# One transpose group and one activation change places in the last stage's instruction order

## The chip, the cores and the metric

The kernel runs on one core of one Trainium2 chip. The metric is the device time of one execution in microseconds (us), measured on the chip. Inside the core, TensorE (PE), VectorE (DVE), ScalarE (ACT), GpSimd (POOL) and SyncE (SP) each run their own list of instructions in the order in which it was written, and they meet only at semaphores.

## The reference

The input x has 16 batches of 256 rows with 256 columns. It passes four residual parts: a decayed running sum gated by x, a feed-forward layer whose operands are quantised to fp4, attention with 16 heads, and a second feed-forward layer whose operands are quantised to block floating point (blocks of 32 share an exponent, 3 mantissa bits). Only the last one matters here:

```python
def block_quant(v, m_bits, bk):              # blocks of bk along the last axis
    amax = max(abs(vb), axis=-1)             # vb: v cut into blocks
    scale = exp2(floor(log2(amax)) - m_bits)
    return round(vb / scale) * scale
h = block_quant(layernorm(x)) @ block_quant(w_fc).T + b_fc       # 256 -> 1024
h = gelu(h)
x = x + tanh(g) * (block_quant(h) @ block_quant(w_proj).T + b_proj)   # 1024 -> 256
```

## The kernel before, in words

All data of the 16 batches stays on the chip between the stages. There are three stages, one after the other: the running sum with the fp4 layer, the attention, and the last feed-forward layer. Each stage is written once per engine as a body for one batch; `over_batches` runs it for batches 0 to 15, the middle ones in a loop of two batches per turn. In the last stage batches 2 to 9 are in that loop. A body works on several batches at once, since it is a software pipeline: `b` is the batch whose hidden values are quantised in this body, `fwd` is b+2, `prv` is b-1.

The way of one batch through the last stage is this. VectorE takes the statistics of its rows (`ff_input_stats`), GpSimd the power, ScalarE normalises (`ff_norm`), VectorE finds block maxima (`ff_input_magic`), GpSimd adds the rounding constant (`ff_input_up`), VectorE subtracts it (`ff_input_codes`). TensorE transposes these codes (`ff_turn_input`, L696), ScalarE copies them out (`ff_input_out`, L999). TensorE multiplies them in four pieces of 512 columns (`ff_fc(b, 0)` to `ff_fc(b, 3)`, L709 and L711), and ScalarE applies gelu to each piece (`ff_gelu(b, u)`, L1005, into `f_h`). VectorE takes the block maxima of all four pieces at once and makes the constants (`ff_hidden_magic`, L1607 to L1614); its wait is for all four gelus: `dve.wait_ge(f_a_gelu, b.count(4, 4))`. GpSimd adds the constants (`ff_hidden_up`, L1214), VectorE subtracts them in two halves (`ff_hidden_codes`, L1623, two instructions). TensorE transposes each half (`ff_turn_hidden(b, 0)` and `(b, 1)`, L724), ScalarE copies each out (`ff_hidden_out`, L1011), TensorE multiplies by the second weights (`ff_proj`, L733 and L736), and VectorE adds the residual (`ff_add_ffn`, L1630).

The transposed input of batch b+3 shares a PSUM bank with the first half of the hidden transposes of batch b. Therefore `ff_turn_input(b+3)` waits until `ff_hidden_out(b, 0)` has copied that half out.

The order of VectorE in the body of b, which the change does not touch, is: the residual of b-2, a small shift for b+5, `ff_hidden_magic(b+1)`, the statistics of b+6, `ff_input_codes(b+3)`, the two halves of `ff_hidden_codes(b)`, `ff_input_magic(b+4)`. So the maxima that follow the gelus of body b (which are those of batch b+2) are the third item of VectorE's body b+1. GpSimd's order is `ff_input_up(b+3)`, `ff_hidden_up(b)`, the power for b+6. SP stores one finished batch per body. GpSimd's `ff_hidden_up(b)` writes a single buffer and so waits for the codes of b-1; `ff_gelu(b+2, 0)` waits for `ff_hidden_up(b)`, since `f_h` has two buffers.

Of the kernel before, what the change touches and what calls it, by code (L numbers as in the profile page):

```python
# [146 lines left out]
def build_main(nc, load, loaded, out_v, g_xattn, g_ffn, w_gate_up, w_down, w_fc, b_fc, w_proj, b_proj, ident, decay,  # L147
# [3 lines left out]
    with ExitStack() as keep:  # L151
# [274 lines left out]
        def _(pe):  # L426
# [260 lines left out]
            def ff_turn_input(b):  # L687
                pe.wait_ge(f_v_code, b.count(1, 1))
                if b.shifted(-1):
                    pe.wait_ge(f_a_x, b.shifted(-1).count(1, 1))  # L690
                if b.shifted(-3):
                    pe.wait_ge(f_a_h, b.shifted(-3).count(C, 1))
                bank = f_ps_x.bitcast(BF16)
                for kc in range(KD):
                    for c in range(C):
                        ins = nc.tensor.transpose(bank[:, (kc * C + c) * P:(kc * C + c + 1) * P],  # L696
                                                  f_xcode[:, b.par, c, kc * P:(kc + 1) * P], idb[:, :])
                ins.then_inc(f_t_x, 1)

            def ff_fc(b, u):  # L700
                c, half = u // 2, u % 2
                cols = slice(half * 512, (half + 1) * 512)
                if u == 0:
                    pe.wait_ge(f_a_x, b.count(1, 1))
                if b.shifted(-1):
                    pe.wait_ge(f_a_gelu, b.shifted(-1).count(4, u + 1))
                elif u >= 2:
                    pe.wait_ge(a_exp, SU * B)
                nc.tensor.matmul(f_ps_fc[u // 2][:, u % 2, :], ones3[:, :], bias3[:, cols], start=True, stop=False)  # L709
                for kc in range(KD):  # L710
                    ins = nc.tensor.matmul(f_ps_fc[u // 2][:, u % 2, :], f_xt[:, b.par, kc, c, :], w_fc_t[:, kc, cols],  # L711
                                           start=False, stop=kc == KD - 1)
                ins.then_inc(f_t_fc, 1)

            def ff_turn_hidden(b, c):
                pe.wait_ge(f_v_hcode, b.count(C, c + 1))
                if c == 0 and b.shifted(2):
                    pe.wait_ge(f_a_x, b.shifted(2).count(1, 1))
                if c == 1 and not b.shifted(-1):
                    pe.wait_ge(a_v_out, len(V_OUT) * B)  # L720
                if b.shifted(-1):
                    pe.wait_ge(f_a_h, b.shifted(-1).count(C, c + 1))
                for k in range(KH1):
                    ins = nc.tensor.transpose(f_ps_h[c][:, :].bitcast(BF16)[:, k * P:(k + 1) * P],  # L724
                                              f_hcode[:, b.par, c, k * P:(k + 1) * P], idb[:, :])
                ins.then_inc(f_t_h, 1)

            def ff_proj(b, c):
                if c == 0 and b.shifted(-1):
                    pe.wait_ge(f_v_y, b.shifted(-1).count(1, 1))  # L730
                if c == 0 and not b.shifted(-1):
                    pe.wait_ge(a_v_out, len(V_OUT) * B)
                nc.tensor.matmul(f_ps_o[:, c, :], ones3[:, :], bias3[:, I1:I1 + D], start=True, stop=False)  # L733
                pe.wait_ge(f_a_h, b.count(C, c + 1))
                for k in range(KH1):
                    ins = nc.tensor.matmul(f_ps_o[:, c, :], f_ht[:, b.par, c, k, :], w_proj_t[:, k, :],  # L736
                                           start=False, stop=k == KH1 - 1)
                ins.then_inc(f_t_o, 1)

            def ff_body(b):  # L740
                prv, fwd = b.shifted(-1), b.shifted(2)
                if fwd:
                    ff_fc(fwd, 0)
                    ff_fc(fwd, 1)
                if prv:
                    ff_proj(prv, 0)
                if fwd:
                    ff_fc(fwd, 2)
                if prv:
                    ff_proj(prv, 1)  # L750
                if fwd:
                    ff_fc(fwd, 3)
                ff_turn_hidden(b, 0)
                if b.shifted(3):
                    ff_turn_input(b.shifted(3))
                ff_turn_hidden(b, 1)
# [36 lines left out]
            for u in range(4):  # L793
                ff_fc(lead[1], u)
            ff_turn_input(lead[2])
            over_batches(pe, ff_body, FFN_AHEAD, FFN_BEHIND)
            ff_proj(last, 0)
            ff_proj(last, 1)

        @block.scalar  # L800
        def _(act):
# [185 lines left out]
            def ff_norm(b):  # L987
                act.wait_ge(f_v_shift, b.count(1, 1))
                if b.shifted(-2):
                    act.wait_ge(f_g_up, b.shifted(-2).count(1, 1))  # L990
                for c in range(C):
                    nc.scalar.activation(f_xn[:, b.par, c * D:(c + 1) * D], tiles(xres, b)[:, c, :], ACT.Identity,
                                         bias=f_shift[:, b.par, c:c + 1], scale=f_rstd[:, b.par, c:c + 1]).then_inc(f_a_norm, 1)

            def ff_input_out(b):
                act.wait_ge(f_t_x, b.count(1, 1))
                if b.shifted(-2):
                    act.wait_ge(f_t_fc, b.shifted(-2).count(4, 4))
                nc.scalar.copy(f_xt[:, b.par].rearrange("p a c t -> p (a c t)"), f_ps_x.bitcast(BF16)).then_inc(f_a_x, 1)  # L999

            def ff_gelu(b, u):
                act.wait_ge(f_t_fc, b.count(4, u + 1))
                if u == 0 and b.shifted(-2):
                    act.wait_ge(f_g_hup, b.shifted(-2).count(1, 1))
                nc.scalar.activation(f_h[:, b.par, u * 512:(u + 1) * 512], f_ps_fc[u // 2][:, u % 2, :], ACT.Gelu).then_inc(f_a_gelu, 1)  # L1005

            def ff_hidden_out(b, c):
                act.wait_ge(f_t_h, b.count(C, c + 1))
                if b.shifted(-2):
                    act.wait_ge(f_t_o, b.shifted(-2).count(C, c + 1))  # L1010
                nc.scalar.copy(f_ht[:, b.par, c].rearrange("p k t -> p (k t)"), f_ps_h[c][:, :].bitcast(BF16)).then_inc(f_a_h, 1)  # L1011

            def ff_body(b):
                fwd = b.shifted(2)
                if fwd:
                    ff_gelu(fwd, 0)
                    ff_gelu(fwd, 1)
                if b.shifted(5):
                    ff_norm(b.shifted(5))
                if fwd:  # L1020
                    ff_gelu(fwd, 2)
                    ff_gelu(fwd, 3)
                ff_hidden_out(b, 0)
                if b.shifted(3):
                    ff_input_out(b.shifted(3))
                ff_hidden_out(b, 1)

            act.dma_start(idf[:, :], ident).then_inc(const_loaded, 16)
# [41 lines left out]
            ff_input_out(lead[2])  # L1070
            ff_norm(lead[4])
            over_batches(act, ff_body, FFN_AHEAD, FFN_BEHIND)

        @block.gpsimd
# [695 lines left out]
```

## Time and profile before

| | |
|---|---|
| median of 3 runs | 823.79 us (823.54 to 824.48) |
| profiled execution, its own time | 823.79 us |
| span of its trace | 821.7 us |
| mean granted TensorE clock | 0.937 |
| busy: PE / DVE / ACT / POOL | 704.8 / 691.7 / 486.3 / 431.6 us |
| last stage | about 669 us to the end of the span |

The span runs from the first instruction to the last; the profiled execution's own time is 2.1 us longer. Busy time is an average over three stages with different limits, so the last stage has to be read by itself.

### The profile page before, as it was taken

To read this page: it belongs to the slowest core of one execution; us is meant where nothing else is said; L and a number is where in the kernel's file an instruction comes from. 1 tells how busy PE (TensorE), PEld (TensorE's weight loads), DVE (VectorE), ACT (ScalarE), POOL (GpSimd) and SP (SyncE) were. 2 spreads that over 40 slices of the span, in tenths; PEclk is the share of its full clock that TensorE was granted. 3 is DMA by queue.
4 is the path that set the end of the run, shared out by engine and by line. 5 is a ranking of instruction groups with operands and counts; after the bars stand their busy time and mean duration, and the time that the engine had idled before them with its cause. 6 is when DMAs were issued, how large, how long until landed. Compare 5 with 4: busy or idle time off the path is not lost.

```text
span 821.7 us, 16554 instructions
## 1 busy us (share of the span) xinstructions
PE 704.8 (86%) x5075; PEld 517.6 (63%) x5090; DVE 691.7 (84%) x1230; ACT 486.3 (59%) x955; POOL 431.6 (53%) x331
## 2 busy tenths in 40 slices
PE   2365999999999998689999999999999876787785
PEld 1254888888888886566666666666666433455454
DVE  6856888888888878878999999998998649999995
ACT  3343455454555442428878887788878684656653
POOL 3623656646566555745444455555443516666553
PEclk9776999999999999889999999999999796989898
DMA  8710000000000000001000000000001000100011
GB/s 275 231 46 0 1 1 1 0 0 0 0 0 1 1 0 2 1 13 41 2 3 2 1 1 1 1 2 1 1 1 53 2 1 0 37 28 26 27 39 52
DMA packets 17719, 18.35 MB, mean 22 GB/s; under 512 B 1670, under 2 KB 16912, under 8 KB 17680
## 3 DMA queue, kind: packets, MB, share of 16 engines
q1 hardware_dynamic: 17084, 17.66, 6.6%
q8 instruction: 21, 0.34, 0.2%
q10 hardware_dynamic: 596, 0.20, 0.1%
q14 instruction: 18, 0.15, 0.1%
HBM read 13.39 MB, written 4.19 MB: 21 GB/s over the span
## 4 chain that ended last, share of the span: by engine, by line
PE 57%; DVE 20%; issue 9%; ACT 5%; POOL 3%; DMA 3%; DVEq 1%; SPq 1%; POOLq 0%; ACTq 0%
PE ps_o L540 9%; PE a_ps_pv L635 7%; PE a_ps_t L579 7%; PE a_ps_s L620 6%; PE a_ps_m L599 5%; DVE f_ps_small L1607 4%; PE ps_gu L504 4%; PE ps_gu L506 4%; PE ps_gu L505 4%; DVE f_hcode L1623 4%; PE a_ps_t L599 3%; DMA ctx<-in_ctx 2%; DVE maxima L1522 2%; PE a_ps_pv L643 1%; ACT stack_t L934 1%
## 5 line engine op out<-in xcount | busy, mean ns | idle before, releaser
L943 ACT ACTIVATE probs<-a_ps_s 128x512 f32<-128x512 f32 x256 | 148.1, 602 | 31.2 <-PE a_ps_s L620 26.6
L1522 DVE TENSOR_REDUCE maxima<-a_ps_m 128x2 f32<-128x512 f32 x160 | 102.8, 683 | 11.1 <-PE a_ps_m L599 10.9
L620 PE MATMUL a_ps_s<-stack_t 64*128 64x256 f32 x512 | 102.3, 315 | 3.9 <-ACT probs L943 1.7
L1165 POOL TENSOR_TENSOR stack<-roped,stack 128x512 f32<-128x512 f32 x32 | 42.8, 1338 | 109.5 <-DVE stack L1512 108.0
L540 PE MATMUL ps_o<-w2t,hqt 128*128 128x256 f32 (+1 forms) x384 | 99.1, 392 | 1.3 <-ACT hqt L871 0.7
L504 PE MATMUL ps_gu<-w1h,yth 128*128 128x352 f32 x256 | 86.9, 340 | 4.5 <-DVE h L1335 4.5
L934 ACT CAST stack_t<-a_ps_t 128x512 fp32r<-128x512 f32 x128 | 71.8, 585 | 31.1 <-PE a_ps_t L579 31.1
L635 PE MATMUL a_ps_pv<-probs,v_aug 128*32 128x256 f32 x1024 | 84.4, 402 | 3.0 <-ACT probs L943 2.9
L579 PE MATMUL a_ps_t<-idf,stack 128*128 128x128 f32 x512 | 76.8, 291 | 8.9 <-POOL stack L1165 5.1
L505 PE MATMUL ps_gu<-w1l,yth 128*128 128x352 f32 x256 | 83.2, 325 | 0.0
L506 PE MATMUL ps_gu<-w1h,ytl 128*128 128x352 f32 x256 | 83.1, 325 | 0.0
L540 PEld LDWEIGHTS ps_o<-w2t,hqt 128*128 128x128 f32 (+1 forms) x384 | 66.3, 189 | 22.1 <-issue 12.4
L620 PEld LDWEIGHTS a_ps_s<-stack_t 64*128 64x128 f32 x512 | 67.9, 190 | 17.0 <-ACT probs L943 9.1
L579 PEld LDWEIGHTS a_ps_t<-idf,stack 128*128 128x128 f32 x512 | 57.9, 146 | 25.4 <-ACT stack_t L934 8.4
L1522 DVE TENSOR_REDUCE maxima<-a_ps_t 128x2 f32<-128x512 f32 x96 | 63.0, 683 | 11.1 <-PE a_ps_t L599 10.9
L1139 POOL TENSOR_TENSOR hq<-hcode,hscale 128x1408 f32<-128x1408 bf16 x16 | 41.5, 2595 | 56.6 <-DVE hcode L1354 56.6
L863 ACT ACTIVATE sg<-ps_gu 128x352 f32<-128x352 f32 x64 | 29.7, 464 | 67.7 <-PE ps_gu L506 67.7
L599 PE MATMUL a_ps_m<-stack_t 64*128 64x256 f32 x320 | 66.0, 322 | 3.8 <-DVE maxima L1522 2.9
L599 PEld LDWEIGHTS a_ps_m<-stack_t 64*128 64x128 f32 x320 | 43.1, 187 | 34.5 <-DVE maxima L1522 18.8
L1214 POOL TENSOR_TENSOR f_hup<-f_h,f_hmag 128x2048 f32<-128x2048 f32 x16 | 58.2, 3640 | 9.1 <-DVE f_hcode L1623 8.1
L1005 ACT ACTIVATE f_h<-f_ps_fc 128x512 f32<-128x512 f32 x64 | 35.2, 595 | 42.5 <-POOL f_hup L1214 38.2
L1335 DVE TENSOR_TENSOR h<-sg,ps_gu 128x352 f32<-128x352 f32 x64 | 33.2, 519 | 28.3 <-ACT sg L863 28.0
(181 smaller groups left out, 1702.7 us busy)
## 6 DMA issues: line engine op xcount, KB each, us to landing
xres<-in_x SPq DMA_DIRECT2D x16, 256.0 KB, 3.2
ctx<-in_ctx SPq DMA_DIRECT2D x16, 256.0 KB, 3.9
out_x<-f_y SPq DMA_DIRECT2D x16, 256.0 KB, 2.1
w1a_raw<-in_w_gate_up SPq DMA_DIRECT2D x1, 1024.0 KB, 5.8
w_raw<-in_w_fc SPq DMA_DIRECT2D x1, 1024.0 KB, 5.5
w_raw<-in_w_proj SPq DMA_DIRECT2D x1, 1024.0 KB, 4.8
w_raw<-in_w_down SPq DMA_DIRECT2D x1, 704.0 KB, 9.3
stack_t<-neg_max_t SPq DMA_DIRECT2D x32, 8.0 KB
```

What stands on the lines that cost most here:

```text
L504: nc.tensor.matmul(into, yth[:, kc, c, :], w1h[:, kc, cols], start=kc == 0, stop=False)
L505: nc.tensor.matmul(into, yth[:, kc, c, :], w1l[:, kc, cols], start=False, stop=False)
L506: ins = nc.tensor.matmul(into, ytl[:, kc, c, :], w1h[:, kc, cols], start=False, stop=kc == KD - 1)
L540: ins = nc.tensor.matmul(ps_o[:, c, :], hqt[0:rows, g, n, :], w2t[0:rows, k, :], start=k == 0, stop=k == KH0 - 1)
L579: ins = nc.tensor.transpose(a_ps_t[:, g % 2, (n * C + c) * P:(n * C + c + 1) * P], a_stack[:, b.par, which, c, 2 * pair:2 * pair + 2, :].r ...
L599: ins = nc.tensor.matmul(max_bank(m)[:, n, :], a_stack_t[b.par][rows, 0, pair, c * P:(c + 1) * P], a_stack_t[b.par][rows, 1, pair, :], sta ...
L620: ins = nc.tensor.matmul(a_ps_s[:, half, n, :], a_stack_t[b.par][rows, 1, pair, kc * P:(kc + 1) * P], a_stack_t[b.par][rows, 0, pair, :], ...
L635: ins = nc.tensor.matmul(a_ps_pv[32 * n:32 * n + 32, quad % 2, 0:T], a_v_aug[:, b.par, kc, 4 * quad + n, :], a_probs[:, (2 * g + n % 2) % ...
L934: nc.scalar.copy(a_stack_t[b.par][:, g % 2, pair:pair + 2, :].rearrange("p a t -> p (a t)"), a_ps_t[:, g % 2, :]).then_inc(a_t, 1)
L943: nc.scalar.activation(a_probs[:, u % 8], a_ps_s[:, u % 2], ACT.Exp).then_inc(a_exp, 1)
L1214: nc.gpsimd.tensor_tensor(f_blocks(f_hup[:, :]), f_blocks(f_h[:, b.par]), f_spread(f_hmag[:, b.par], F_NBH), ALU.add).then_inc(f_g_hup, 1)
L1522: nc.vector.tensor_reduce(a_maxima[:, b.par, c, 4 * quad + half:4 * quad + half + 3:2], max_bank(m), X, ALU.max).then_inc(a_v_max, 1)
```

## The change

In the body of TensorE in the last stage, `ff_turn_hidden(b, 0)` goes ahead of `ff_fc(fwd, 3)`. In the body of ScalarE, `ff_gelu(fwd, 3)` goes behind `ff_hidden_out(b, 0)` and `ff_input_out(b+3)`, ahead of `ff_hidden_out(b, 1)`. Nothing is added or removed; the semaphores and their counts stay.

```diff
@@ TensorE, ff_body
                 if prv:
                     ff_proj(prv, 1)
+                ff_turn_hidden(b, 0)
                 if fwd:
                     ff_fc(fwd, 3)
-                ff_turn_hidden(b, 0)
                 if b.shifted(3):
                     ff_turn_input(b.shifted(3))
                 ff_turn_hidden(b, 1)
@@ ScalarE, ff_body
                 if fwd:
                     ff_gelu(fwd, 2)
-                    ff_gelu(fwd, 3)
                 ff_hidden_out(b, 0)
                 if b.shifted(3):
                     ff_input_out(b.shifted(3))
+                if fwd:
+                    ff_gelu(fwd, 3)
                 ff_hidden_out(b, 1)
```

## Rows read from the trace of the kernel before

**Rows 1.** Busy time by stretch: the loop, then bodies, cut where VectorE's hidden codes start.
```profile
core 0: us, PE busy (x) PEld busy (x) DVE busy (x) ACT busy (x) POOL busy (x), PEclk, DMA share, GB/s
704.00:777.00 73.00, 57.00 (x397) 35.48 (x404) 68.52 (x125) 44.61 (x74) 44.76 (x24) 0.88 0.08 29
...
694.25:703.44 9.19, 7.60 (x62) 5.19 (x62) 8.54 (x18) 6.06 (x11) 5.77 (x4) 0.98 0.09 30
703.44:712.48 9.04, 7.21 (x57) 4.56 (x56) 8.45 (x17) 5.36 (x10) 5.67 (x4) 1.00 0.08 30
712.48:721.89 9.41, 6.86 (x37) 4.06 (x37) 8.54 (x18) 5.90 (x11) 5.79 (x4) 0.64 0.08 28
...
767.06:775.64 8.58, 7.03 (x59) 4.94 (x59) 8.28 (x12) 5.42 (x10) 5.30 (x3) 1.00 0.09 32
...
792.94:799.10 6.16, 4.49 (x39) 2.80 (x39) 5.66 (x7) 4.21 (x7) 3.64 (x1) 1.00 0.12 43
799.10:805.35 6.25, 5.61 (x52) 4.19 (x51) 5.69 (x6) 4.07 (x6) 3.64 (x1) 1.00 0.13 44
```

**Rows 2.** VectorE in order of time: start us, duration us; bodies 1 to 3.
```profile
698.73 2.28 DVE L1607 TENSOR_REDUCE f_ps_small<-f_h 128x64 f32<-128x2048 f32 x1
...
703.44 2.35 DVE L1623 TENSOR_TENSOR f_hcode<-f_hup,f_hmag 128x1024 bf16<-128x1024 f32 x2
...
706.88 0.75 DVE L1630 SCALAR_TENSOR_TENSOR f_y<-f_ps_o,gates,xres 128x512 f32<-128x512 f32 x1
...
707.62 2.29 DVE L1607 TENSOR_REDUCE f_ps_small<-f_h 128x64 f32<-128x2048 f32 x1
...
717.18 2.28 DVE L1607 TENSOR_REDUCE f_ps_small<-f_h 128x64 f32<-128x2048 f32 x1
```

**Rows 3.** TensorE and ScalarE in order of time, body 2.
```profile
704.50 1.07 ACT L1005 ACTIVATE f_h<-f_ps_fc 128x512 f32<-128x512 f32 x2
...
704.71 0.62 PE L724 MATMUL f_ps_h<-idb,f_hcode 128*128 128x128 bf16 x8
705.46 1.02 ACT L1011 COPY f_ht<-f_ps_h 128x1024 bf16<-128x1024 bf16 x1
...
706.62 0.38 PE L696 MATMUL f_ps_h<-idb,f_xcode 128*128 128x128 bf16 x4 [1.29 <-ACT f_ht L1011]
...
707.13 0.59 ACT L999 COPY f_xt<-f_ps_h 128x512 bf16<-128x512 bf16 x1 [0.65 <-PE f_ps_h L696]
...
707.61 1.02 ACT L1011 COPY f_ht<-f_ps_h 128x1024 bf16<-128x1024 bf16 x1
```

**Rows 4.** GpSimd in order of time, the hidden addition of batch 3.
```profile
707.99 3.64 POOL L1214 TENSOR_TENSOR f_hup<-f_h,f_hmag 128x2048 f32<-128x2048 f32 x1
```

**Rows 5.** The first body (0) in order of time, TensorE, VectorE and ScalarE.
```profile
686.87 1.04 PE L724 MATMUL f_ps_h<-idb,f_hcode 128*128 128x128 bf16 x8 [5.36 <-DVE f_hcode L1623]
...
689.09 2.29 DVE L1607 TENSOR_REDUCE f_ps_small<-f_h 128x64 f32<-128x2048 f32 x1
689.10 0.59 PE L696 MATMUL f_ps_h<-idb,f_xcode 128*128 128x128 bf16 x4 [1.19 <-ACT f_ht L1011]
...
689.72 0.59 ACT L999 COPY f_xt<-f_ps_h 128x512 bf16<-128x512 bf16 x1 [0.77 <-PE f_ps_h L696]
```

**Rows 6.** Bodies 12 and 13 in order of time, TensorE, ScalarE and VectorE.
```profile
794.20 0.62 PE L724 MATMUL f_ps_h<-idb,f_hcode 128*128 128x128 bf16 x8 [0.20 <-DVE f_hcode L1623]
...
794.86 1.01 ACT L1011 COPY f_ht<-f_ps_h 128x1024 bf16<-128x1024 bf16 x1 [0.22 <-PE f_ps_h L724]
...
796.44 0.59 ACT L999 COPY f_xt<-f_ps_h 128x512 bf16<-128x512 bf16 x1 [0.56 <-PE f_ps_h L696]
...
795.87 2.28 DVE L1607 TENSOR_REDUCE f_ps_small<-f_h 128x64 f32<-128x2048 f32 x1
...
801.85 0.60 ACT L1005 ACTIVATE f_h<-f_ps_fc 128x512 f32<-128x512 f32 x1 [1.03 <-PE f_ps_fc L711]
...
802.54 2.29 DVE L1607 TENSOR_REDUCE f_ps_small<-f_h 128x64 f32<-128x2048 f32 x1 [0.42 <-ACT f_h L1005]
```

## The prediction

> **What bounds the kernel now.** The change touches only the last stage, so I read that stage and leave the first 669 us alone: no instruction there moves, and the statement order ahead of the stage's first body is the same. I read the busy time by stretch first, then the order of time of each engine in one body, then the first body and the last bodies, since those have other neighbours.
>
> In the loop VectorE is busy 68.52 of 73.00 us, TensorE 57.00, ScalarE 44.61 and GpSimd 44.76 [rows 1]. The reader should see that one engine is full and three are not. A body lasts as long as VectorE needs: I cut the stage at each start of the hidden codes, and the seven bodies 2 to 8 take from 703.44 to 767.06, 63.62 us, or 9.09 each. They alternate between two lengths, of which 9.04 and 9.41 are shown [rows 1]; the long one holds the jump back of the two-batch loop. From body 9 on VectorE has no statistics left to take and the body is 8.58 [rows 1]; there GpSimd's addition of 3.64 us [rows 4] sits in the cycle with VectorE's codes and sets the length. In bodies 12 and 13 even less is left, 6.16 and 6.25 [rows 1].
>
> So VectorE is the engine that loses time if anything makes it wait. What matters is when its reductions over the hidden values (2.28 us each) may begin, since they need all four gelus. In body 2 the codes start at 703.44 and the next reduction at 707.62, 4.18 later; in body 3 they start at 712.48 and the reduction at 717.18, 4.70 later [rows 1, 2]. The pattern repeats: 4.18 in the four even bodies of the seven, 4.68 to 4.70 in the three odd ones. In both cases VectorE comes to the reduction by its own order (the residual addition at 706.88 and a small shift are right ahead of it) and the gelus are long done: the pair with the fourth gelu ends at 704.50 + 1.07 = 705.57, 2.05 us before the reduction [rows 2, 3]. This 2.05 us is all the slack that the fourth gelu has.
>
> **Part one: TensorE turns the first half of the hidden codes ahead of the fourth fc piece.** No work is added. The transposes wait for VectorE's first half of codes; in body 2 they start at 704.71, 1.27 after the codes began, and last 0.62 [rows 2, 3]. The piece of fc that now stands behind them is three matmuls. It fits into the 1.29 us in which TensorE sits idle between these transposes and those of the input [rows 3], so the input's transposes aren't late at full clock. Queued behind the waiting transposes are that fc piece, the input's transposes and the second half; only the fc piece waits longer than before, and only the fourth gelu reads it. Cost by itself: nothing; its cover is that idle gap. In the first body, where the transposes run at half clock (1.04 us) [rows 5], the fc piece may end up to 0.15 us after the copy, and I keep that as a part of the upper bound.
>
> **Part two: ScalarE does the fourth gelu behind two copies.** This is where the time goes. The fourth gelu used to need only its matmuls. Now it stands behind the copy of the first hidden half, which needs the codes of this body, and behind the copy of the input, which needs transposes that in turn need the first copy. I add up this chain from the start of the hidden codes:
>
> - codes start to transposes: 1.27 [rows 2, 3]
> - transposes to the hidden copy: 0.66 when ScalarE is free [rows 6], 0.75 in body 2 where it was still at the gelu [rows 3]; I take 0.70
> - hidden copy to the input's transposes: 706.62 - 705.46 = 1.16 [rows 3]
> - those to the input copy: 707.13 - 706.62 = 0.51 [rows 3]
> - input copy to the next instruction of ScalarE: 707.61 - 707.13 = 0.48 [rows 3]
> - one gelu 0.59 (half of a pair with its overlap; 0.60 alone [rows 6]), and 0.09 from its end to the start of the waiting reduction: 802.54 - (801.85 + 0.60) [rows 6]
>
> The sum is 4.80 us. VectorE used to reach its reduction at 4.18 or 4.70. So it now waits 0.62 us in the even bodies and 0.10 in the odd ones; in the odd ones the jump back of VectorE's loop simply falls into the wait. What follows the reduction (its constants, statistics, input codes, then the next hidden codes) hangs on it as before: 4.71 from 698.73 to 703.44 [rows 2]. Nothing gives that time back, because the chain starts again at the next codes: it is now a closed cycle VectorE, TensorE, ScalarE, TensorE, ScalarE, VectorE of 4.80 + 4.71 = 9.51 us against a mean of 9.09. For bodies 2 to 8: 4 x 0.62 + 3 x 0.10 = 2.78 us.
>
> The copy of the second hidden half moves back by one gelu, 0.5 us, from 707.61 [rows 3]. Only the second projection of the next body reads it, and VectorE needs that product a whole body later still (its residual is that of b-2); behind that projection TensorE has the transposes, which wait for VectorE's codes anyway. I count nothing; without this cover it could cost its own 0.5 us in a body. GpSimd's addition starts at 707.99 and ends at 711.63, 0.85 ahead of the codes at 712.48 [rows 1, 4]; it doesn't depend on the delayed reduction of the same time (that one serves the addition a body later), so it stays where it is and gets more slack.
>
> **The first two bodies.** In body 0 the input copy starts at 689.72; the gelu behind it lets the reduction start at 689.72 + 0.48 + 0.59 + 0.09 = 690.88, where it was 689.09 [rows 5]. With 4.71 behind it the codes of batch 1 start at 695.59 instead of 694.25: 1.34 us. Part of the 1.79 is absorbed, since in this body the codes waited for GpSimd anyway. In body 1 the reduction came 698.73 - 694.25 = 4.48 after the codes [rows 1, 2]; now 4.80, so 0.32 more.
>
> **The last bodies.** In bodies 9 to 11 the new cycle is shorter than GpSimd's, because the statistics are gone: 4.80, and from the reduction to the codes about 1.3 less than 4.71, is 8.2, under the 8.58 there [rows 1]. Nothing is added. In body 12 the next codes come after only 6.16 us and the reduction began at 795.87, before the input copy at 796.44 [rows 6]. Now it has to wait for that copy and the gelu: 796.44 + 1.16 = 797.60. From reduction to codes it takes 805.35 - 802.54 = 2.81 [rows 1, 6], so the codes of batch 13 come at 800.41 instead of 799.10: 1.31 us. In body 13 there is no input copy: 1.26 + 0.66 + 0.90 (the copy of 1.01 with 0.11 overlap, as the input copy has) + 0.59 + 0.09 = 3.50, and 2.81 more: 806.72 instead of 805.35, together 1.37 us. Bodies 14 and 15 have no gelu; they keep that shift and add nothing.
>
> **Sum**: 1.34 + 0.32 + 2.78 + 0 + 1.37 = 5.81 us. The profiled execution's own time is 823.79 (span 821.7 and 2.1 around it), and the median of the runs is the same, so the forecast is 829.6 us.
>
> The clock of TensorE is the unknown. The three bodies shown of 1 to 3 have granted clocks of 0.98, 1.00 and 0.64 [rows 1], and in body 0 the transposes take the half clock's time [rows 5]: parts of some bodies run at 1.2 GHz, half of the 2.4. The falls came after TensorE's waits around the transposes. At the half clock the chain's own two groups of transposes cost 1.04 - 0.62 and 0.59 - 0.38 more, 0.63 us [rows 3, 5 and 6]. Until now that was hidden; in the new cycle it isn't. I take none in the sum, since the shown body that falls does so only behind its first transposes, and keep up to 8 x 0.63 = 5.0 us as the upper end. The Trainium skill, page "TensorE: Matmul & The Clock Gate", section on the clock gate, says that the engine's default is the halved clock and that activity releases it. By that rule a longer body with the same matmuls would make half clock more common than these rows show, and the time would be nearer to the second rival's 834.6 than to my sum; the fc piece that now splits the idle gap speaks the other way. No row of before can tell which.
>
> **The rivals.**
> 1. *GpSimd's cycle keeps the period in the loop too.* If VectorE's wait were taken up by slack that I don't see, bodies 2 to 8 would cost nothing, and only the head and the tail stay: 1.34 + 0.32 + 1.37 = 3.0, 826.8 us. For it: in body 9 GpSimd's cycle is 8.58. Against it: in the loop its addition is done 0.85 before the codes [rows 1, 4], and VectorE has no gap of 0.6 us ahead of the codes to give.
> 2. *The half clock falls on the new cycle in nearly every body*: 829.6 + 5.0 = 834.6 us. For it: the granted clock of the whole loop is 0.88, and 0.64 in body 3 [rows 1]. Against it: in body 2, at a clock of 1.00, both groups of transposes ran at full speed [rows 3], and the fall of body 3 took only a part of it.
> 3. *Nothing measurable.* The gelu reaches the reduction in time nearly everywhere, 823.8 us. That needs the chain of 4.80 to be wrong by 0.6 and the tail's by more.
> 4. *Faster.* The transposes no longer queue behind the fc piece and the copy no longer behind the gelu, so the hidden and input copies come earlier and VectorE's remaining gaps close. The place is VectorE in the loop; the most it could give is its idle time there, 73.00 - 68.52 = 4.5 us, 819.3 us. It decides if the chain to the reduction is under 4.18 us. For it: in body 2 the hidden copy did start 0.09 later than it could. Against it: the six terms of the chain were read in one stretch and exceed 4.18 by 0.62, and VectorE didn't wait for either copy before.
>
> **How the numbers follow.** The sum as it stands, with some cold transposes in a few bodies, is 828 to 832: 0.73. Rival 1: 0.08. Rival 2, and any other larger loss: 0.10. Rival 3: 0.05. Rival 4: 0.04. The range 826.5 to 832.8 leaves out rivals 2, 3 and 4, 0.19 together. A change under 0.2% (1.6 us) can't be told from none in this kernel; so faster 0.04, same 0.05, slower 0.91.
>
> **What would show it.** In the profile after: VectorE's reduction (L1607) has idle time in front of it, ended by ScalarE's gelu, in nearly every body, about 0.6 us in the even ones; the time between codes and reduction is near 4.8 in both kinds of body; the distance between codes is 9.4 to 9.6 in bodies 2 to 8, unchanged 8.6 in 9 to 11, and about 7.5 in body 12. The idle time of the hidden copies and of TensorE in front of the input's transposes stays about the same in sum. The prediction is wrong if that idle time is absent, if body 12 stays near 6.2, or if the reduction's wait ends at anything other than the gelu.

## The result: 0.8% slower, by VectorE's wait for the fourth gelu

The changed kernel takes 831.47 us (median of 6 runs, 828.79 to 832.40), the kernel before 823.66 beside it. The ratio is 1.0077 with an interval of 1.0059 to 1.0095. Timed again, beside other runs, it was 830.51 against 824.10, ratio 1.0074 (1.0051 to 1.0097). The forecast was 829.6 and slower. The profiled execution took 830.41, with a span of 828.3 against 821.7, so 6.6 us are to be found in its trace.

The waits of VectorE in the last stage (from 669 us on) name the cause. The columns are who waited for whom, us in total, times, and the longest.

```profile
DVE f_ps_small L1608 <- ACT f_h L1005: 10.2, 13, 1.8
...
DVE f_hcode L1624 <- POOL f_hup L1215: 3.2, 1, 3.2
DVE f_y L1631 <- PE f_ps_o L736: 2.2, 1, 2.2
DVE f_y L1631 <- issue: 2.0, 4, 0.6
```

The first line is new: the reduction over the hidden values waits for ScalarE's gelu in 13 of its 16 instances, where it had waited once, 0.42 us [rows 6]. It is 10.2 us and the kernel lost 6.6. In bodies 0 and 9 to 11 a part of the wait only takes the place of time that VectorE had spent on its input codes (`ff_input_codes`), which were drawn out beside GpSimd's addition: they take 0.69 us in the loop, and in body 9 they took 1.65 before and 0.88 after. In body 12 it takes the place of a wait of 0.36 us for that addition, and at the end 1.5 us came back. The input codes of body 9, before:

```profile
774.07 1.65 DVE L1599 TENSOR_TENSOR f_xcode<-f_xup,f_xmag 128x512 bf16<-128x512 f32 x1
```

and after:

```profile
781.47 0.88 DVE L1600 TENSOR_TENSOR f_xcode<-f_xup,f_xmag 128x512 bf16<-128x512 f32 x1
```

Next, the same stretches as before, cut again where the hidden codes start. Columns: stretch; its length; busy us of PE, PEld, DVE, ACT and POOL; granted clock; DMA share; GB/s.

```profile
685.94:695.87 9.93, 7.61 (x50) 4.91 (x50) 7.79 (x16) 6.44 (x12) 5.75 (x4) 0.75 0.00 0
695.87:705.42 9.55, 7.59 (x50) 4.54 (x50) 8.64 (x17) 5.13 (x9) 5.78 (x4) 0.82 0.09 29
705.42:715.30 9.88, 7.97 (x42) 4.50 (x43) 8.56 (x18) 5.96 (x11) 5.67 (x4) 0.65 0.08 27
715.30:724.71 9.41, 7.28 (x60) 4.63 (x58) 8.54 (x18) 5.07 (x9) 5.78 (x4) 1.00 0.08 28
734.13:744.17 10.04, 7.63 (x50) 4.80 (x50) 8.64 (x18) 6.16 (x11) 5.78 (x4) 0.83 0.07 26
705.42:773.69 68.27, 52.06 (x350) 32.01 (x350) 60.01 (x114) 38.98 (x64) 40.01 (x22) 0.85 0.08 27
773.69:782.26 8.57, 6.68 (x46) 4.28 (x47) 7.59 (x12) 4.52 (x8) 5.29 (x3) 0.80 0.10 33
799.57:807.07 7.50, 5.46 (x45) 3.51 (x46) 5.68 (x8) 5.48 (x10) 3.64 (x1) 1.00 0.11 37
807.07:813.42 6.35, 4.79 (x44) 3.10 (x42) 5.68 (x7) 2.79 (x4) 3.64 (x1) 1.00 0.12 41
819.59:828.30 8.71, 3.38 (x34) 2.53 (x34) 3.77 (x4) 2.02 (x2) 0.00 (x0) 0.95 0.18 62
```

The loop (bodies 2 to 8) and the last stretch of the kernel before, in the same columns:

```profile
703.44:767.06 63.62, 49.56 (x339) 30.61 (x344) 59.44 (x113) 38.39 (x64) 40.02 (x22) 0.87 0.08 29
...
811.52:821.70 10.18, 4.86 (x34) 3.57 (x34) 3.77 (x4) 2.02 (x2) 0.00 (x0) 0.79 0.15 53
```

Against these and [rows 1], by place:

| place | before | after | difference | forecast |
|---|---|---|---|---|
| ahead of the first hidden codes | 685.60 | 685.94 | +0.34 | 0 |
| body 0 | 8.65 | 9.93 | +1.28 | +1.34 |
| body 1 | 9.19 | 9.55 | +0.36 | +0.32 |
| bodies 2 to 8 | 63.62 | 68.27 | +4.65 | +2.78 |
| bodies 9 to 11 | 25.88 | 25.88 | 0 | 0 |
| body 12 | 6.16 | 7.50 | +1.34 | +1.31 |
| body 13 | 6.25 | 6.35 | +0.10 | +0.06 |
| body 14 | 6.17 | 6.17 | 0 | 0 |
| last codes to the end | 10.18 | 8.71 | -1.47 | 0 |
| sum, up to rounding | | | +6.6 | +5.81 |

The first line is no effect: these codes began between 684.45 and 688.13 in the traces of this study. Two lines differ much from the forecast, bodies 2 to 8 and the end, and both come with TensorE's clock. VectorE in order of time, bodies 4 and 6 of the changed kernel:

```profile
724.71 2.35 DVE L1624 TENSOR_TENSOR f_hcode<-f_hup,f_hmag 128x1024 bf16<-128x1024 f32 x2
...
728.16 0.75 DVE L1631 SCALAR_TENSOR_TENSOR f_y<-f_ps_o,gates,xres 128x512 f32<-128x512 f32 x1
...
729.50 2.29 DVE L1608 TENSOR_REDUCE f_ps_small<-f_h 128x64 f32<-128x2048 f32 x1 [0.53 <-ACT f_h L1005]
...
744.17 2.35 DVE L1624 TENSOR_TENSOR f_hcode<-f_hup,f_hmag 128x1024 bf16<-128x1024 f32 x2
...
747.62 0.75 DVE L1631 SCALAR_TENSOR_TENSOR f_y<-f_ps_o,gates,xres 128x512 f32<-128x512 f32 x1
...
749.58 2.29 DVE L1608 TENSOR_REDUCE f_ps_small<-f_h 128x64 f32<-128x2048 f32 x1 [1.15 <-ACT f_h L1005]
```

From codes to reduction it is 4.79 us in body 4, the predicted 4.80, and 5.41 in body 6. The chain of body 6, TensorE and ScalarE, shows why:

```profile
745.44 1.03 PE L724 MATMUL f_ps_h<-idb,f_hcode 128*128 128x128 bf16 x8 [2.24 <-DVE f_hcode L1624]
...
746.60 1.01 ACT L1011 COPY f_ht<-f_ps_h 128x1024 bf16<-128x1024 bf16 x1 [1.70 <-PE f_ps_h L724]
...
747.75 0.59 PE L696 MATMUL f_ps_h<-idb,f_xcode 128*128 128x128 bf16 x4
...
748.46 0.58 ACT L999 COPY f_xt<-f_ps_h 128x512 bf16<-128x512 bf16 x1 [0.85 <-PE f_ps_h L696]
748.94 0.61 ACT L1005 ACTIVATE f_h<-f_ps_fc 128x512 f32<-128x512 f32 x1
```

The two groups of transposes take 1.03 and 0.59 us where full clock gives 0.62 and 0.38 [rows 3]: 0.62 us more, which is all of 5.41 - 4.79. The granted clock from 745.44 to 746.47 is 0.50, which is 1.2 GHz. TensorE had been idle for 2.24 us in front of the first group; in body 4 it had been idle for 2.22 us and the group still took 0.62, so the idle time alone does not tell which body is hit. This price was named in the prediction, but left out of its sum.

### The profile page after: what moved, and what is told of

Read it like the earlier page. It is cut to its first block, busy times and chain, and to the rows that moved or that the text cites. A ratio compares the mean times of both kernels' runs of the same rounds, so it can differ in the third digit from the quotient of the medians.

```text
span 828.3 us, 16569 instructions
## 1 busy us (share of the span) xinstructions
PE 706.1 (85%) x5090; PEld 516.6 (62%) x5090; DVE 689.9 (83%) x1230; ACT 485.8 (59%) x955; POOL 430.8 (52%) x331
## 4 chain that ended last, share of the span: by engine, by line
PE 58%; DVE 18%; issue 9%; ACT 8%; POOL 4%; DMA 1%; POOLq 0%; DVEq 0%; ACTq 0%; SPq 0%
PE ps_o L540 9%; PE a_ps_pv L635 7%; PE a_ps_t L579 7%; PE a_ps_s L620 6%; PE a_ps_m L599 5%; DVE f_ps_small L1608 4%; PE ps_gu L504 4%; PE ps_gu L506 4%; PE ps_gu L505 4%; PE a_ps_t L599 3%; DVE f_hcode L1624 2%; DVE maxima L1523 2%; PE a_ps_pv L643 1%; ACT stack_t L934 1%; ACT probs L943 1%
```

## The experiments

Each was timed in five rounds beside the kernel before on the same chip. The two parts of the change came first.

**ScalarE's part alone.**

```diff
 ScalarE: gelu(fwd, 2)
-         gelu(fwd, 3)
          hidden_out(b, 0); input_out(b+3)
+         gelu(fwd, 3)
 TensorE: as in the kernel before
```

> Only ScalarE's part of the change: the fourth gelu stands behind the two copies, TensorE keeps its old order. Theory (VectorE's reduction waits for a closed chain through transposes, hidden copy, input transposes, input copy and the fourth gelu): the loss is all here, 5.8 to 7.8 us over the kernel before, 829.5 to 831.5, and VectorE's idle time in front of its hidden reduction, ended by the gelu, is about 10 us in sum. Rival (TensorE's new order, with a longer idle stretch ahead of the transposes, brings the half clock and with it a part of the loss): the transposes run at full clock more often than with the whole change and the loss is 5.5 us or less. Second rival (the two parts cost only together): under 1 us.

829.99 us against 824.44, ratio 1.0070 (1.0053 to 1.0087). VectorE's wait for the gelu is 9.2 us, body 0 takes 9.92, body 12 7.70, and bodies 2 to 8 take 67.30 together (68.27 with the whole change). So ScalarE's order is enough for most of the loss, and by the medians it can't be told from the whole. That the parts cost only together is out.

The rival that gives TensorE's new order a share, through the half clock, is not out. The mean clock of the loop is 0.85 in either order, but this trace differs in where the half clock falls. Body 6, the same group of hidden transposes that took 1.03 us above:

```profile
743.54 0.62 PE L724 MATMUL f_ps_h<-idb,f_hcode 128*128 128x128 bf16 x8 [1.67 <-DVE f_hcode L1624]
```

Here this group took 0.61 to 0.62 us in all seven bodies 2 to 8, with 1.67 us of idle time in front of it at most. In both traces of the changed kernel it took 0.88 to 1.04 us in three of the seven, and the seven bodies took 1.0 and 1.2 us more. The loss, 5.6 us by the medians, lies on the border between what the theory and this rival had named. How often the half clock falls there in the runs without a trace is not shown.

**TensorE's part alone.**

```diff
 TensorE: proj(prv, 1)
+         turn_hidden(b, 0)
          fc(fwd, 3)
-         turn_hidden(b, 0)
 ScalarE: as in the kernel before
```

> Only TensorE's part: the first hidden transposes go ahead of the fourth fc piece, ScalarE keeps its old order. Theory: the fourth gelu now ends some 3.5 us after the start of the hidden codes, under the 4.18 at which VectorE comes to its reduction, so the loop doesn't change; in body 12 it may be 0.3 us late: within 0.5 us of the kernel before, 823.3 to 824.3. Rival (the order on TensorE costs through its clock): 1.5 to 3 us slower.

828.35 us against 824.44, ratio 1.0057 (1.0037 to 1.0076). My expectation missed, and it was the prediction's step "cost by itself: nothing". The profiled execution (span 825.4) shows where. TensorE and ScalarE, with VectorE's reduction, in body 12, whose codes begin at 794.49:

```profile
796.60 0.61 PE L724 MATMUL f_ps_h<-idb,f_hcode 128*128 128x128 bf16 x8
...
797.05 0.38 PE L709 MATMUL f_ps_fc<-bias,ones 128*128 128x512 bf16 x1
797.26 0.59 PE L711 MATMUL f_ps_fc<-w_fc_t,f_xt 128*128 128x512 bf16 x2
...
797.90 0.60 ACT L1005 ACTIVATE f_h<-f_ps_fc 128x512 f32<-128x512 f32 x1 [1.48 <-PE f_ps_fc L711]
...
798.60 2.29 DVE L1607 TENSOR_REDUCE f_ps_small<-f_h 128x64 f32<-128x2048 f32 x1 [1.04 <-ACT f_h L1005]
```

TensorE reaches the transposes 2.11 us after the codes began, not 1.27, because the projection in front of them ends late. Each instruction put ahead of the fc piece then delays the fourth gelu directly.

The lateness has a source in the new order itself. ScalarE still has its copy of the hidden half behind the fourth gelu, and that gelu now needs a piece of fc that stands behind the transposes. So the copy starts late, and with it the input's transposes, which need its bank. Body 11 of the kernel before:

```profile
786.37 0.61 PE L724 MATMUL f_ps_h<-idb,f_hcode 128*128 128x128 bf16 x8
...
788.22 0.38 PE L696 MATMUL f_ps_h<-idb,f_xcode 128*128 128x128 bf16 x4 [1.24 <-ACT f_ht L1011]
```

and of this run:

```profile
788.68 0.61 PE L724 MATMUL f_ps_h<-idb,f_hcode 128*128 128x128 bf16 x8
...
791.62 0.38 PE L696 MATMUL f_ps_h<-idb,f_xcode 128*128 128x128 bf16 x4 [1.68 <-ACT f_ht L1011]
```

From one group to the other it is 2.94 us instead of 1.85. The half clock has a share too: the pairs of fc matmuls that start at 783.31 and 784.57 took 1.04 and 1.06 us, where at full clock a pair takes 0.59. VectorE's reduction waits 1.04 us in body 12 and 1.04 in body 13, and the two bodies take 6.91 and 7.92 us instead of 6.16 and 6.25. That is 2.4 of the 3.2 us that the stage lost in this trace; 0.3 more fell in body 0, the last stretch gave 0.3 back, and 0.8 fell in bodies 2 to 8, in two of which TensorE was at half clock and late. In the whole change none of this shows: the copy no longer stands behind the gelu (1.90 us from group to group in body 4), and the gelu waits longer for the copies anyway. The median lost 3.9 us, some 0.7 more than this one execution explains.

**TensorE's new order in bodies 2 to 9 alone** was run last, to test that reading.

```diff
 TensorE, only where b is in the two-batch loop:
+         turn_hidden(b, 0)
          fc(fwd, 3)
-         turn_hidden(b, 0)
```

> TensorE's new order in the loop bodies 2 to 9 alone, the old one at both ends, ScalarE's old order everywhere. Theory (TensorE's part alone costs because the fourth fc piece, and the gelu with it, comes 1.1 us later where TensorE reaches the transposes late, which is in bodies 12 and 13, and in the loop only where TensorE runs at half clock): body 12 and 13 are back at 6.2 us each, bodies 2 to 8 take 63.6 to 64.4 together, and the kernel is 0 to 0.9 us slower than before. Rival (the order costs a little in every body): 2 us or more slower, with bodies 2 to 8 over 65.

824.64 us against 824.00, ratio 1.0009 (1.0000 to 1.0019). Bodies 2 to 8 take 63.64 us, as before, and VectorE waits only the old 0.42 us for a gelu. TensorE's input transposes are late there too (2.94 to 2.95 us behind the first group), but in the loop VectorE's slack covers it. So nearly all that the order costs it costs through the bodies outside the loop.

**The gelu one place earlier.**

```diff
 ScalarE, changed kernel:
          hidden_out(b, 0)
+         gelu(fwd, 3)
          input_out(b+3)
-         gelu(fwd, 3)
```

> The changed kernel with the fourth gelu one place earlier on ScalarE: behind the first hidden copy, ahead of the input copy. Theory: the chain from codes to reduction is 1.27 + 0.66 + 0.90 + 0.59 + 0.09 = 3.5 us, under 4.18, so VectorE waits nowhere in the loop and the time is 0 to 1 us over the kernel before (0.2 to 0.5 in bodies 12 and 13), 823.7 to 824.7. Rival (standing behind the copy of hidden values is what costs, not the round trip to TensorE for the input): most of the loss stays, 4 us or more.

824.43 us against 824.44, ratio 0.9999 (0.9984 to 1.0014). VectorE's waits for the gelu in the last stage:

```profile
DVE f_ps_small L1608 <- ACT f_h L1005: 2.3, 3, 1.0
```

Three waits are left (bodies 0, 12 and 13) and none in the loop, where the reduction starts 4.18 and 4.70 us after the codes as in [rows 1, 2]. Body 12 takes 6.35 and body 13 6.78, 0.7 us more than before together. This settles which link costs: standing behind the hidden copy is free, a 3.5 us chain under VectorE's 4.18, and it even hides TensorE's part at the ends for the most. The round trip of the input, to TensorE and back, makes it 4.8 and dear.

**The clock on the new cycle.**

```diff
 TensorE, changed kernel:
          proj(prv, 1)
+         if fwd: wait for the last fourth gelu, then
+                 6 more 128x512 bias matmuls into the fourth piece's bank
          turn_hidden(b, 0)
          fc(fwd, 3)
```

> The changed kernel with six more 128x512 bias matmuls in every body on TensorE, in its idle stretch ahead of the first hidden transposes (they write the bank of the fourth fc piece, which that piece then overwrites). Theory (what the changed kernel lost beyond the 5.8 us of the sum is the half clock on the chain's transposes): these transposes run at full clock nearly everywhere, bodies 2 to 8 take about 9.5 each instead of 9.75, and the time is 2 to 3 us under that of the changed kernel, 828.5 to 829.7. Rival (the excess has another cause): no less than the changed kernel, or more, by the fillers' own 1.3 us where TensorE is late.

829.01 us against 824.44, ratio 1.0054 (1.0037 to 1.0071), where the changed kernel itself had 1.0077 and 1.0074. The same columns as above, bodies 2 to 8, 9 to 11, 12 and 13:

```profile
703.74:769.91 66.17, 52.23 (x394) 31.47 (x392) 59.88 (x113) 38.98 (x65) 40.04 (x22) 1.00 0.08 28
769.91:795.78 25.87, 21.90 (x167) 13.27 (x166) 23.29 (x32) 14.76 (x24) 14.60 (x7) 1.00 0.09 32
795.78:803.28 7.50, 6.33 (x50) 3.71 (x48) 5.68 (x7) 5.47 (x10) 3.64 (x1) 1.00 0.10 35
803.28:810.21 6.93, 5.78 (x50) 3.81 (x48) 5.68 (x7) 2.79 (x4) 3.64 (x1) 1.00 0.12 40
```

At a granted clock of 1.00 bodies 2 to 8 take 66.17 us, 2.55 more than before; the forecast for them was 2.78. So the new cycle at full clock costs nearly what the sum said, and the remaining 2.10 of the 4.65 is the half clock. The fillers have a price of their own where TensorE is late: 6.93 instead of 6.35 in body 13. The Trainium skill, page "TensorE: Matmul & The Clock Gate", section on the clock gate, has it that activity releases the halved clock, and this trace agrees: 2.1 us came back through matmuls whose results nobody reads. The ratios with and without the fillers, taken in different comparisons, have overlapping intervals; the trace shows the effect more clearly than the medians do.

**By place.** The changed kernel was run again beside the next three.

> The changed kernel once more, to stand beside the next three on the same chip. 5 to 8 us over the kernel before; bodies 2 to 8 between 66.2 (all at full clock) and 69 us together, against 63.6.

830.51 us against 824.10; bodies 2 to 8 take 68.45 us in its trace.

```diff
 both engines: the new order where b is 0, 1 or 10 to 15,
               the old one in the loop (2 to 9)
```

> The new order on both engines only in the bodies outside the loop (0, 1 and 10 to 15), the old order in bodies 2 to 9. Theory (the sum of the prediction by place): body 0 takes about 9.95 and body 12 7.5 us, bodies 2 to 8 stay at 63.6 together, and the kernel is 3.0 us slower than before, somewhat less than half of the whole loss. Rival (the loss is in the loop only): under 1 us. Rival (the loss is mostly at the ends): 5 us or more.

826.24 us against 824.10, ratio 1.0024 (1.0009 to 1.0040). Its bodies 0, 2 to 8, 12, and the last codes to the end:

```profile
686.09:696.02 9.93, 7.58 (x50) 4.91 (x50) 7.79 (x17) 6.44 (x12) 5.75 (x4) 0.76 0.00 0
705.61:769.23 63.62, 48.19 (x344) 31.17 (x349) 59.46 (x113) 38.42 (x63) 40.03 (x22) 0.87 0.08 29
795.11:802.61 7.50, 5.23 (x44) 3.51 (x46) 5.68 (x8) 5.47 (x10) 3.64 (x1) 1.00 0.12 37
815.13:823.90 8.77, 3.38 (x34) 2.53 (x34) 3.77 (x4) 2.02 (x2) 0.00 (x0) 1.00 0.18 62
```

The head and the tail lose what the prediction gave them, body by body, and the loop nothing: 63.62 to the digit. The expected 3.0 us are there up to body 13 (3.1). The end gives 1.4 back at full clock (8.77 against 10.18), which makes the measured 2.1 us plausible, with 3.0 inside the interval.

**The jump of the two-batch loop.** The last stage was written out for all 16 batches, once with each order.

```diff
 over_batches, last stage only:
-    with eng.Fori(head, B // 2 - tail) as j: ...
+    for j in range(B // 2): body(Batch(j, 0)); body(Batch(j, 1))
```

> The kernel before with the last stage written out for all 16 batches, without the two-batch loop. Theory (in the loop VectorE is the bound, and its jump back costs about 0.52 us in each of four turns): the odd bodies fall from 9.4 to 8.8, 2.1 us less, 821.5 to 822.5. Rival (loading the longer instruction lists costs what the jump did): the same time or slower.

821.88 us against 824.10, ratio 0.9973 (0.9959 to 0.9986): 2.2 us faster. Six of the seven bodies 2 to 8 take 8.7 us now, instead of 8.8 and 9.4 in turn, and one 9.1.

> The changed kernel with the last stage written out in the same way. Theory (the new cycle through the fourth gelu sets the period, and VectorE's jump back lies in its wait for that gelu): bodies 2 to 8 stay at 9.4 to 9.5 at full clock, the time is within 0.7 us of the changed kernel, and its distance from the unrolled kernel before grows to about 8 us. Rival (VectorE's own work still sets the odd bodies): it falls by the same 2 us as the kernel before.

829.50 us against 824.10 and 1.0 under the changed kernel beside it, where at most 0.7 was expected; the unrolled kernels lie 7.6 us apart. VectorE in order of time, one former odd body:

```profile
716.50 2.35 DVE L1629 TENSOR_TENSOR f_hcode<-f_hup,f_hmag 128x1024 bf16<-128x1024 f32 x2
...
719.89 0.75 DVE L1636 SCALAR_TENSOR_TENSOR f_y<-f_ps_o,gates,xres 128x512 f32<-128x512 f32 x1
...
721.21 2.29 DVE L1613 TENSOR_REDUCE f_ps_small<-f_h 128x64 f32<-128x2048 f32 x1 [0.50 <-ACT f_h L1010]
...
725.82 2.35 DVE L1629 TENSOR_TENSOR f_hcode<-f_hup,f_hmag 128x1024 bf16<-128x1024 f32 x2
```

The jump is gone, and in its place stand 0.50 us of wait; the body is 9.32 against 9.41, where the same body of the kernel before fell from 9.41 to 8.73. So the jump did fall into the wait. Bodies 2 to 8 take 65.97 us together, 2.3 less than in the changed kernel. Only a part of that is the jump: in this trace the first hidden transposes took 0.62 to 0.63 us in every one of these bodies, as with ScalarE's part alone.

**The end of the kernel.**

```diff
 TensorE, kernel before, bodies 14 and 15:
+         4 and 8 more 128x512 bias matmuls (in 14 behind a wait for the last gelu)
          turn_hidden(b, 0)
```

> The kernel before with four and eight more 128x512 bias matmuls on TensorE ahead of the first hidden transposes of bodies 14 and 15 (into a bank that nothing reads any more). Theory (the stretch from the last hidden codes to the end takes 10.2 us in the kernel before and 8.7 in the changed one only because its transposes and projections fall to the half clock in the one and not in the other): that stretch comes to 8.7 us and the kernel is 1 to 1.4 us faster. Rival (the stretch differs through its waits, not its clock): it stays at 10.2 and the time is the same within 0.3 us.

In the profiled execution the last stretch fell as expected: the last codes begin at 812.71 and the span ends at 821.4, so 8.7 us at a granted clock of 1.00, against 10.18. The median is 823.26 against 823.96, ratio 0.9994 (0.9983 to 1.0004). That is less than expected and can't be told from no change. Whether the runs without a profile fall to the half clock at the end as often as this trace of before does was not seen.

**A version that beats both.**

```diff
 last stage written out; gelu(fwd, 3) in its old place; fillers as above
 TensorE, body 13:  fc(15, 0..3), then proj(12, 0), proj(12, 1)
 VectorE, body 14:  hidden_magic(15), then the residual of 12
```

> The version that the runs point to: the old order of the gelu, the last stage written out, the fillers of the run before, and in body 13 all four fc pieces ahead of the two projections with the reduction of batch 15 ahead of the residual of batch 12 on VectorE. Theory: 2.1 us from the loop's jumps, 1.4 from the clock at the end and about 1 from body 13 (7.35 us in the unrolled kernel, 6.3 now): 4 to 4.5 us faster than before, 819.5 to 820.3. Rival (the loss of body 13 is not TensorE's lateness): body 13 stays over 7 and the kernel is 3 us faster at most.

820.92 us against 823.96, ratio 0.9961 (0.9947 to 0.9974), 3.0 us faster than before and, by the ratios, some 9 us faster than the changed kernel. From the unrolled kernel before (0.9973) it can't be told: the intervals overlap. The codes of batches 13 and 14 now begin at 796.59 and 802.78, 6.19 us apart instead of 7.35 in the first unrolled kernel. That fits TensorE's lateness as the loss there, but the new orders on TensorE and on VectorE were not tried apart. The sum of 4 to 4.5 us was too high. A part of the excess is at the end, which takes 9.24 us here and not 8.7, with all its matmuls at full clock. The last codes begin at 808.96, and TensorE then does this:

```profile
809.17 1.89 PE L768 MATMUL f_ps_fc<-bias,ones 128*128 128x512 bf16 x8
...
810.90 1.09 PE L729 MATMUL f_ps_h<-idb,f_hcode 128*128 128x128 bf16 x16
```

The fillers came late and pushed the transposes back: they start 1.94 us after the codes, where in the run before it was 1.29 (814.00 - 812.71).

## Why the prediction was right, and where its sizes were off

- **VectorE is the bound and the fourth gelu's slack is 2.05 us.** Right. The new wait is VectorE's, at the reduction, ended by the gelu.
- **The chain of 4.80 us from codes to reduction.** Right at full clock for the even bodies: 4.79 in body 4. With the clock held at 1.00 bodies 2 to 8 lost 2.55 us, where 2.78 was forecast. The difference lies in the odd bodies: in that trace their reductions start 4.70 to 4.71 us after the codes, as before, and not 4.80, so they lose 0.01 to 0.02 us each where 0.10 was forecast. The part from the reduction to the next codes did not change (4.6 to 4.9 us in both).
- **No half clock in the sum.** This is the mis-sized term. It measured 2.1 us in the profiled execution. The argument was one body [rows 3] whose transposes ran at full clock. Two things were missed. Putting the transposes on a cycle that had hidden them turns every fall of the clock on them into time. And the falls came onto them more often: in bodies 2 to 8 of the kernel before the first group, the hidden transposes, took 0.61 to 0.62 us in all seven, and the input's group was slow in two (0.58 and 0.46 us). In the changed kernel the first group was slow in three (0.88 to 1.04 us) and the input's in five (0.58 to 0.59). Added up over full clock that is 0.28 us before and 2.12 after. The mean clock of the loop (0.87 and 0.85) does not show this. What brings the falls there stays open. TensorE now waits 1.96 to 2.24 us in front of the first group in six of the seven bodies, where it had waited 1.19 at most; but in the unrolled changed kernel it waited up to 2.36 us and that group took 0.63.
- **Head and tail.** Right to 0.06 us in each body: 1.28 for 1.34, 0.36 for 0.32, 1.34 for 1.31, 0.10 for 0.06, and nothing in bodies 9 to 11, where GpSimd's cycle keeps 8.6.
- **TensorE's part costs nothing.** Wrong alone (3.9 us). Two steps failed. The input's transposes do get late, by 1.1 us in body 11, since with ScalarE's old order the hidden copy waits for the gelu of the delayed piece; I had said that only the fc piece waits longer. And where the slack is least, in bodies 12 and 13, TensorE comes late to the transposes and the gelu is waited for; these bodies should have been read for this step too. Inside the whole change neither shows, apart from the share that the half clock may have by this order.
- **The end.** Not foreseen: 1.47 us came back in the last stretch, whose granted clock was 0.95 against 0.79. I didn't look at the clock there at all. That the sum of 5.81 came so near to the 6.6 of the traces is in part luck: the loop lost 1.87 us more than forecast, and the end gave nearly as much back.
- **Rivals.** GpSimd as the bound of the loop was wrong there and right in bodies 9 to 11. Half clock in every body was too much: five of the loop's seven bodies were long in the profile, at 9.6 to 10.0, and two stayed at 9.4. The other two did not occur.

## What to carry to other kernels

Before an instruction goes behind another on an in-order engine, add up what that other waits for, link by link, up to the consumer of the moved one, and compare it with the time at which the consumer arrives today: here 4.80 against 4.18 cost 0.8% and 3.5 against 4.18 cost nothing. Do it for the short bodies at the ends as well, where the slack is least. And once a chain passes through TensorE's short groups, price them at both clocks, by the rows of the groups themselves: a mean clock of a whole loop does not show on which groups the falls lie. When the order of one engine alone is changed, ask also what stands behind the delayed result on the other: TensorE's part alone held up a copy on ScalarE, and through it TensorE.

## What the runs showed that was not expected

The end of the kernel, from the last hidden codes on, took 8.7 to 8.8 us in all six traces with the fourth gelu behind the input copy in the last bodies, and in the kernel before with fillers at the end. Its granted clock was 0.95 to 1.00 in these. It took 9.55 to 10.21 us in five others, at 0.77 to 0.83, and 9.24 in the last version, where the fillers themselves held it up. Fillers apart, the instructions are the same. What in the preceding two bodies decides the clock stays open. Unrolling brought a trap of its own: in body 13 of the unrolled kernel before, fc(15, 0) began at half clock behind the transposes of body 12, the fourth piece came late, and the body took 7.35 us instead of 6.25, half of what the jumps had given.
